# A Trainium2 kernel of attention and feed-forward layers: GpSimd's feed-forward operations tile by tile, attention's sums cleared there, a norm moved behind the last inner tile

## What is computed

```python
# layer 1: a mixture of experts on x (two of eight experts), gives x1
# layer 2: linear attention with kv sums, then this feed-forward part
x2 = layer_norm(x1 + attn, g1, b1)
gate = x2 @ Wg + bg                  # 256 -> 682
up = x2 @ Wu + bu
ffn = (silu(gate) * up) @ Wd + bd    # 682 -> 256
y = x + layer_norm(x2 + ffn, g2, b2)
# layer 3: softmax attention, 16 heads of 16, keys that the mask marks are left out
q, k, v = y @ Wq.T, y @ Wk.T, y @ Wv.T
scores = where(mask, -inf, q k^T * scale)
out = softmax(scores) v
# then Wo, an RMS norm, shift and scale by the condition
# layer 4: a mixture of experts with 16 experts and a shared one, added to y
```

## Time and profile before

| what | value |
|---|---|
| median of 3 runs | 913.29 us (911.43 to 913.87) |
| profiled execution | 911.58 us, its span 909.9 us |
| PE busy | 821.8 us (90%) |
| DVE busy | 695.6 us (76%) |
| POOL busy | 398.4 us (44%) |
| ACT busy | 362.5 us (40%) |
| granted TensorE clock, mean | 0.96 |

### The profile page before, as it was taken

The page is one execution under the profiler, slowest core; times in us unless marked ns, Lnnn a source line. Parts: engine busy times, 40 slices in busy tenths (PEclk is TensorE's granted clock), DMA queues, the critical chain, the costliest instruction groups (busy, mean ns, idle before and its releaser), DMA issues. The chain is left out here.

```text
span 909.9 us, 17077 instructions
## 1 busy us (share of the span) xinstructions
PE 821.8 (90%) x5386; PEld 736.3 (81%) x5386; DVE 695.6 (76%) x1399; ACT 362.5 (40%) x722; POOL 398.4 (44%) x435
## 2 busy tenths in 40 slices
PE   7799999999994688769999889887999999999997
PEld 4699999999994567657887779865888888888887
DVE  4888888888882578887788879787686777777776
ACT  5466655566650555243331545683111111111110
POOL 4277777877773300036654436502232333323232
PEclk9899999999997699788999999999999999999999
DMA  8436314223512600007000020010000010010002
GB/s 292 130 98 202 127 46 123 62 64 124 174 44 81 201 0 1 1 0 222 1 1 1 1 71 1 3 35 1 18 28 24 17 35 17 17 35 17 17 0 93
DMA packets 45912, 55.20 MB, mean 61 GB/s; under 512 B 5166, under 2 KB 34920, under 8 KB 45864
## 3 DMA queue, kind: packets, MB, share of 16 engines
q1 hardware_dynamic: 41384, 43.59, 15.2%
q0 software_dynamic: 4032, 11.02, 3.9%
q10 hardware_dynamic: 448, 0.01, 0.0%
HBM read 47.00 MB, written 7.60 MB: 60 GB/s over the span
## 5 line engine op out<-in xcount | busy, mean ns | idle before, releaser
L2109 POOL TENSOR_TENSOR kTh<-at_acc,kTh 128x512 fp32r<-128x512 f32 x68 | 88.1, 1295 | 231.9 <-DVE kTh L2224 231.9
L1892 PE MATMUL psum<-act_hi,ff_w 128*128 128x512 f32 x544 | 180.3, 392 | 0.4 <-ACT at_acc L2057 0.4
L2057 ACT ACTIVATE at_acc<-psum 128x512 f32<-128x512 f32 x68 | 40.6, 599 | 237.4 <-PE psum L1892 237.4
L1892 PEld LDWEIGHTS psum<-act_hi,ff_w 128*128 128x128 f32 x544 | 102.6, 189 | 21.1 <-ACT at_acc L2057 0.8
L1933 PEld LDWEIGHTS psum<-ff_w,kTh 128*128 128x128 f32 x816 | 106.4, 190 | 8.8 <-DVE y L2305 3.2
L2305 DVE SCALAR_TENSOR_TENSOR y<-psum,ff_rawd,y 128x256 f32<-128x256 f32 x272 | 112.2, 475 | 0.2 <-issue 0.2
L1933 PE MATMUL psum<-ff_w,kTh 128*128 128x256 f32 x816 | 108.4, 283 | 3.1 <-DVE y L2305 3.1
L1892 PE MATMUL psum<-act_lo,ff_w 128*128 128x512 f32 x272 | 106.9, 393 | 0.0
L470 ACT ACTIVATE e_u<-psum,e_bias 128x256 f32<-128x256 f32 x152 | 63.5, 471 | 95.3 <-PE psum L375 84.2
L2221 DVE TENSOR_TENSOR at_acc<-psum,at_acc 128x512 f32<-128x512 f32 x68 | 47.0, 691 | 71.0 <-PE psum L1892 58.6
L774 PE MATMUL psum<-act_hi,ff_w 128*128 128x512 f32 x192 | 64.7, 412 | 6.2 <-DVE ff_h32sb L1506 4.5
(11 more groups left out here) (444 smaller groups left out, 2335.4 us busy)
## 6 DMA issues: line engine op xcount, KB each, us to landing
e_raw<-in_W SPq DMA_DIRECT2D x16, 512.0 KB, 6.5
e_raw<-in_W SPq DMA_DIRECT2D x8, 1024.0 KB, 5.8
v_tok<-in_xT SPq DMA_DIRECT2D x4, 512.0 KB, 9.4
y<-in_x SPq DMA_DIRECT2D x4, 512.0 KB, 10.2
y<-y_rows SPq DMA_DIRECT2D x4, 512.0 KB, 7.3
v_tok<-y_rows SPq DMA_DIRECT2D x4, 512.0 KB, 8.1
v_tok<-in_x SPq DMA_DIRECT2D x4, 512.0 KB, 7.5
e_raw<-in_w_gate SPq DMA_DIRECT2D x16, 128.0 KB, 2.2
```

Source lines behind the costliest of these rows:

```text
L1892: last = pe.matmul(bank[:, :], e2_w[par][a][:, o + k * H2:o + (k + 1) * H2], actT[b][:, k, g * GT:(g + 1) * GT], start=n == 0, stop=n == 3 ...
L2057: act.activation(sl_sb[:, s % 2, :], ps[s % 2][:, :], ACT.Silu).then_inc(esil, 1)
L2109: pool.tensor_tensor(hh[1][:, s % HS, :], h32[:, s % 2, :], hh[0][:, s % HS, :], ALU.subtract).then_inc(hsp, 1)
```

## The change

GpSimd's operations over four tiles in the feed-forward stage (bias and shift rows, the third group's gain and join) become four operations over one tile each, with the signal on the last; the low halves of the key and value weights become two each. The third group's gain and join wait for all 24 low parts (`hsp`) and all shift adds, and the weights' low halves move behind the second join of the last group. TensorE turns the third group behind the third tile of the last `down` instead of the second, and ScalarE's and VectorE's splits of it move with it. The sums of attention are cleared in the feed-forward stage, one of 16 parts after each low part of steps 6 to 21, and their last column is written at the stage's end; TensorE's wait in attention counts that. Query products 4, 5 and 6 go to banks 4, 5 and 3 instead of 3, 4 and 5, and the wait for VectorE's split of part 3 moves from the start of attention's loop to ahead of part 6. Some small tiles are placed inside others, and `acc` is allocated for the whole kernel (not shown).

```diff
--- before.py
+++ after.py
@@ query_bank @@
-            return ps[(0, 1, 2, 3, 3, 4, 5, 7)[u]]
+            return ps[(0, 1, 2, 3, 4, 5, 3, 7)[u]]
@@ stage_feed_forward, tensor: down(g) @@
                             last.then_inc(ops, 1)
                             if g == L1 - 1 and j == 0:
                                 count_keys()
-                            if g == L1 and j == 1:
+                            if g == L1 and j == TG - 2:
                                 turn(g - 1)
@@ stage_feed_forward, scalar @@
                         act.activation(rstd[:, i:i + 1], rstd[:, i:i + 1], ACT.Sqrt).then_inc(root, 1)
-                        if i == L1 * TG + 1:
+                        if i == NT - 2:
                             hi(L1 - 1)
@@ stage_feed_forward, gpsimd @@
                         if g == 1 and m == 2:
                             constants()
+                        if FC <= s < NS - 2:
+                            pool.memset(at.acc[:, s - FC, :, :], 0.0).then_inc(cleared, 1)
                         if m % 2 and s < 4 * G:
 
                             r = s // 2 // 2
-                            sl = slice(r * TG, (r + 1) * TG)
                             if s // 2 % 2 == 0:
                                 pool.wait_ge(gin, 48)
-                                pool.tensor_tensor(y[:, sl, :], y[:, sl, :], group_rows(gb[:, 2, :]), ALU.add).then_inc(biased, 1)
+                                for i in range(r * TG, (r + 1) * TG):
+                                    last = pool.tensor_tensor(y[:, i, :], y[:, i, :], gb[:, 2, :], ALU.add)
+                                last.then_inc(biased, 1)
                             else:
                                 pool.wait_ge(xin[r], 16)
-                                pool.tensor_tensor(xk[:, sl, :], xk[:, sl, :], group_rows(gb[:, 1, :]), ALU.add).then_inc(xbiased, 1)
-                    sl = slice((L1 - 1) * TG, L1 * TG)
+                                for i in range(r * TG, (r + 1) * TG):
+                                    last = pool.tensor_tensor(xk[:, i, :], xk[:, i, :], gb[:, 1, :], ALU.add)
+                                last.then_inc(xbiased, 1)
                     pool.wait_ge(scaled, L1)
-                    pool.tensor_tensor(y[:, sl, :], y[:, sl, :], group_rows(gb[:, 0, :]), ALU.mult).then_inc(gained, 1)
+                    pool.wait_ge(xbiased, G)
+                    pool.wait_ge(hsp, NS)
+                    for i in range((L1 - 1) * TG, L1 * TG):
+                        last = pool.tensor_tensor(y[:, i, :], y[:, i, :], gb[:, 0, :], ALU.mult)
+                    last.then_inc(gained, 1)
                     pool.wait_ge(gained, 1)
-                    pool.wait_ge(xbiased, L1)
-                    pool.tensor_tensor(y[:, sl, :], y[:, sl, :], xk[:, sl, :], ALU.add).then_inc(joined, 1)
-                    for n, home in enumerate((at.wk, at.wv)):
-                        pool.wait_ge(at.weights, n + 1)
-                        pool.tensor_tensor(home[1], pj_raw[:, n + 1, :, :], home[0], ALU.subtract).then_inc(at.wsp, 1)
-                    pool.wait_ge(xbiased, G)
+                    for i in range((L1 - 1) * TG, L1 * TG):
+                        last = pool.tensor_tensor(y[:, i, :], y[:, i, :], xk[:, i, :], ALU.add)
+                    last.then_inc(joined, 1)
                     for j in range(TG - 1):
+                        if j == TG - 2:
+                            for n, home in enumerate((at.wk, at.wv)):
+                                pool.wait_ge(at.weights, n + 1)
+                                for k in range(KC):
+                                    last = pool.tensor_tensor(home[1][:, k, :], pj_raw[:, n + 1, k, :], home[0][:, k, :], ALU.subtract)
+                                last.then_inc(at.wsp, 1)
                         i = L1 * TG + j
                         pool.wait_ge(spread, j + 1)
                         pool.tensor_tensor(y[:, i, :], y[:, i, :], xk[:, i, :], ALU.add).then_inc(joined, 1)
+                    pool.wait_ge(at.penned, 1)
+                    pool.wait_ge(cleared, NI)
+                    pool.tensor_tensor(at.acc[:, :, :, HD].rearrange("p (b u) h -> p b u h", b=B),
...
@@ stage_feed_forward, vector @@
                         norm_last(j)
-                        if j == 1:
+                        if j == TG - 2:
                             lo(L1 - 1)
@@ stage_attention, tensor @@
-                        if i < 2:
-                            pe.wait_ge(qlo, j * QB + QB + i + 1)
+                        if i == 0:
+                            pe.wait_ge(qlo, j * QB + NQP - 1)
...
-                        if i == 0:
-                            pe.wait_ge(qlo, j * QB + NQP - 1)
...
-                    pe.wait_ge(at.ready, B + 1)
+                    pe.wait_ge(at.ready, B + 2)
                     n_blocks = live_blocks(pe)
                     with pe.Fori(0, n_blocks) as j:
                         pe.wait_ge(added, j * NI + 2)
-                        pe.wait_ge(qlo, j * QB + QB)
                         pe.wait_ge(ptc, j * NI + 2)
                         for u in range(QB, QB + KC):
                             query_product(pe, wq, u, qps)
                         project_keys(j)
                         project_values(j, 0)
+                        pe.wait_ge(qlo, j * QB + QB)
                         query_product(pe, wq, NQP - 2, qps)
@@ stage_attention, gpsimd @@
-                    pool.memset(acc[:, :, :, :], 0.0).then_inc(cleared, 1)
-                    pool.wait_ge(at.penned, 1)
-                    pool.wait_ge(cleared, 1)
-                    pool.tensor_tensor(acc[:, :, :, HD].rearrange("p (b u) h -> p b u h", b=B),
...
```

More of the change, by code:

```diff
@@ L1268, in stage_feed_forward @@
             at_ones, counts_ps, seen = (sem(f"ff_{x}") for x in ("ones", "countsps", "seen"))
-            gained, joined, inverted, spread = (sem(f"ff_{x}") for x in ("gained", "joined", "inverted", "spread"))
+            cleared, gained, joined, inverted, spread = (sem(f"ff_{x}") for x in ("cleared", "gained", "joined", "inverted", "spread"))
             n0 = turns_done[0]
@@ L1494, in _ @@
                         pool.tensor_tensor(y[:, i, :], y[:, i, :], xk[:, i, :], ALU.add).then_inc(joined, 1)
+                    pool.wait_ge(at.penned, 1)
+                    pool.wait_ge(cleared, NI)
+                    pool.tensor_tensor(at.acc[:, :, :, HD].rearrange("p (b u) h -> p b u h", b=B),
+                                       at.pen[:, :].unsqueeze(1).unsqueeze(3).to_broadcast([P, B, QT, NH]),
+                                       at.one[:, 0:1].unsqueeze(2).unsqueeze(3).to_broadcast([P, B, QT, NH]), ALU.mult).then_inc(at.ready, 1)
                 @block.vector
@@ L1646, in stage_attention @@
         def stage_attention(q_hi, homes, mask_rows, mask_home, v_tok, wq, qps, qhi, at, load_ahead, pre, loaded, e2_raw, e2_in):
-            mb_set, cleared = sem("at_maskset"), sem("at_cleared")
+            mb_set = sem("at_maskset")
+            acc = at.acc
             qlo, wk, wv, q_lo, z, ks, pT, xt = at.qlo, at.wk, at.wv, at.q_lo, at.z, at.ks, at.pT, at.xt
@@ L1679, in stage_attention @@
                 mb = sbl("at_mb", [P, QT, KB], BF16)
-                acc = sbl("at_acc", [P, NI, NH, HD + 1])
                 mn, df, rc = (sbl(f"at_{x}", [P, NI, NH]) for x in ("mn", "df", "rc"))
@@ L2061, in _ @@
                 def _(pool):
-                    pool.memset(acc[:, :, :, :], 0.0).then_inc(cleared, 1)
-                    pool.wait_ge(at.penned, 1)
-                    pool.wait_ge(cleared, 1)
-                    pool.tensor_tensor(acc[:, :, :, HD].rearrange("p (b u) h -> p b u h", b=B),
-                                       at.pen[:, :].unsqueeze(1).unsqueeze(3).to_broadcast([P, B, QT, NH]),
-                                       one[:, 0:1].unsqueeze(2).unsqueeze(3).to_broadcast([P, B, QT, NH]), ALU.mult).then_inc(cleared, 1)
-                    pool.wait_ge(cleared, 2)
                     def move(j, i):
@@ L2353, in adaln_block @@
         kept, mid = KC * B * HC * KB, KC * T
+        mask_end = [(rows_of.stop - rows_of.start) * (S // 4) for rows_of in mask_rows]
+        raw_line = [v[:, :, :].rearrange("p k n -> p (k n)") for v in ff_raw]
+        lists = top2[:, :, :].rearrange("p i n -> p (i n)")
         at_homes = (ff_raw[0][:, :, :].rearrange("p k n -> p (k n)"), ff_raw[1][:, :, :].rearrange("p k n -> p (k n)"), rawd_line)
@@ L2359, in adaln_block @@
             own8, own4 = sb("at_own8", [P, HC]), sb("at_own4", [P, HB])
-            rank, keys, lv, rb, srt = (sb(f"at_{x}", [P, NKB]) for x in ("rank", "keys", "lv", "rb", "srt"))
-            cnt, pen, nl = sb("at_cnt", [P, QT]), sb("at_pen", [P, QT]), sb("at_nl", [P, 1])
+            keys, lv, rb, srt = (lists[:, n * NKB:(n + 1) * NKB] for n in range(4))
+            rank, cnt, pen = (raw_line[0][:, o:o + n] for o, n in ((mask_end[0], NKB), (mask_end[0] + NKB, QT), (mask_end[0] + NKB + QT, QT)))
```

(4 more changed lines are left out.)

## The result

The changed kernel took 905.67 us (median of 6 runs, 903.81 to 907.32); the kernel before, beside it on the same chip, took 912.59 us (911.43 to 913.96). The ratio is 0.9924, 95% interval 0.9906 to 0.9941: 6.9 us less. The forecast was 907.0 with 903.0 to 912.0, and faster. The profiled execution took 907.32 us with a span of 905.6, the slowest of the six.

A forecast was written before the change was run, and what follows sets the result against it. TensorE sets the feed-forward stage, so only its holes, waits on VectorE, count. +1.1 - 1.5 - 2.4 - 2.85 - 0.65 = -6.3 us takes 911.58 to 905.3, or 907.0 on the median's scale; range 903.0 to 912.0.

The forecast's parts named there:

- A: Group 0, ahead of the first inner product: split GpSimd adds lengthen its queue, +1.1 us (bounds 0 and +1.4).
- B: Group 1, hole at 456.3: VectorE gets turns between short adds, and the later 0.4 us hole goes, -1.5 us.
- C: Group 2, hole at 485.3: same chain shortens the hole and the clock stays up behind it, -2.4 us.
- D: Last group: with the norm behind all low parts, the second query product no longer waits, -2.85 us.
- E: Attention's start: TensorE's first product no longer waits for VectorE's L805 to end, -0.65 us (bounds 0 and -0.75).
- one hole near 1 us: Expected sign ahead of the first inner product: a new hole near 1 us; above 2 us the prediction is wrong.
- The clears: Feed-forward stage: 16 small GpSimd clears, 5 us where it idles 56, taken as nothing beyond B and C.
- The first (the split buys nothing): Groups 1 and 2: GpSimd's queued adds run through, VectorE waits for all four; 911.7 us, chance 0.13.
- The second (the low clock moves): New or shifted holes bring a half-clock stretch, 1.5 us each, perhaps twice; 908.5 to 910.0 us, chance 0.20.
- The third rival: Last group: VectorE's turns stretch the norm's eight operations, TensorE's turn waits, 1.6 us comes back; 908.6 us, chance 0.10.
- The fourth (each handover loses 0.2 us): Short GpSimd operations and clears each lose 0.2 us, all felt by TensorE: +12, 919 us, chance 0.07.
- a handover of about 115 ns: Some eight handovers of the shared resource in A to C would add 0.9 us, making 907.9; left out.

The follow-up runs named there:

- experiment 6: The changed kernel with group 0's two row adds (bias and shift) wide again, one operation each: 904.82 us, ratio 0.9908 against the kernel before.
- Experiment 10: The changed kernel with VectorE's first attention signal ahead of its loading of the block count instead of behind it: 906.50 us, ratio 0.9942 against the kernel before.
- experiment 1: The kernel before with only the eight bias and shift row adds split tile by tile: 908.93 us, ratio 0.9959.
- the three parts alone: The kernel before with only the row adds split (908.93 us), only the third group's norm and turn moved (908.47), or only attention's wait and banks changed (911.98).

## Why the prediction was right, point by point

From the profiled execution's 911.58 us the sum gave 905.3, 6.3 us less. Laid over each other at the stage's start, the traces differ by 6.37 us at attention's first product and by 6.43 at the end. Mechanism and size were right part by part, with the misses named below. (The lower end of the range counts another 4 us for A, B and C, where their own bounds add up to 3.5.)

**A, forecast +1.1, measured +0.82.** The queue on GpSimd was read rightly, and the wide group 0 of experiment 6 takes back 0.85. The short operations alone were priced at 0.8; the 0.3 added for the fourth hidden tile isn't seen in the sum, though 0.82 is itself good only to a few tenths. The cost doesn't stand in one hole near 1 us, as the prediction's signs had it, but in two: 0.53 us ahead of an up product and 0.36 ahead of the first inner product.

**B, forecast -1.5, measured -1.58.** The hole shrank by 1.39 where 1.15 was forecast, the 0.4 us hole went as said, and the inner product came 3.08 us behind the up product.

**C, forecast -2.4, measured -2.53.** The hole gave 1.42 (forecast 1.15), the full clock behind it 1.34 (3.10 us from the up product to the inner product instead of 4.44; forecast 1.54, less the 0.3 for a late low part). About 0.2 us came back until the first up product behind down(2); what that is was not followed.

**D, forecast -2.85, measured -2.88.** Cast and low part took 0.43 and 0.69 us, the last multiply waited for its up product alone, and the norm ended 0.9 us before its transposes (forecast 0.8).

**E, forecast -0.65, measured -0.35,** of which 0.15 is lost between the start of the last down and the end of the stage, so the table shows -0.20; what took it was not followed. The mechanism was right and the term too large: TensorE starts 0.39 us after L805 does, a limit that the trace of before could not show, and the prediction took a value near the other end of its bounds. Experiment 10 shows that the signal isn't what is left.

**The clears, forecast nothing beyond B and C, measured 1.04.** B and C did count the clear ahead of the adds. They did not count that a clear behind a low part lengthens the held cast (1.68 us, above the 1.2 that the prediction gave as the most). On the other side the two holes came out 0.79 and 0.75 us where the forecast left 1.0 each. Two misses of opposite sign, each near half a microsecond, stand inside B and C.

**The rivals.** The first (the split buys nothing) fell on the cast of 0.81 us. The second (the low clock moves) did not happen in either trace of the changed kernel, where D has closed the hole of 2.58 us; experiment 1, with this hole open, shows it happening at 1.47 us. That D is the reason rests on that one trace. The two parts are not independent: the three parts alone give 3.88 + 2.82 + 0.45 = 7.15 us from I to T, near the 7.19 of the whole, but only since the first contains a low stretch (1.47 lost) that the whole doesn't have, and lacks the clears (1.04) that it has. With both put in the parts come to 7.6. That the sum of parts agreed is partly chance. The third rival (the turn waits) fell on the margin of 0.9 us. The fourth (each handover loses 0.2 us): alone, a group's four adds take 2.82 us, the cast 0.43, L1251 1.22 and L1252 at least 1.08, 5.55 or more in all; taking turns, everything from the first add's start to the last add's end took 4.96. An operation that was held ends sooner after its release than a free one takes: the later adds after about 0.6 us (free 0.73), L1251 after 1.08 (free 1.22).

The prediction weighed a handover of about 115 ns, which the Trainium skill's page "SBUF — State Buffer", section "A bandwidth-pool intuition that's wrong", gives for a DMA whose descriptors GpSimd can't write while VectorE holds the ports, and which made 907.9. The held cast of 457.99 ended 0.28 us behind the end of the clear, as the earlier trace rows had 0.29; no run here shows the extra. The sum without it came out at 6.3 against 6.37, but with misses of half a microsecond in it, so the sum alone would not decide.

**The median.** The profiled spans differ by only 4.3 us, since this execution of the changed kernel reached the stage 2.2 us later. The medians differ by 6.9, near the 6.43 of the stage and all behind it. The runs of one kernel spread over 3.5 us; of the changed kernel's, those at 903.8 and 904.0 us have a mean granted clock of 0.966, the profiled one 0.958.

## What to carry to other kernels

Ask of a long GpSimd operation not only how wide it is but which VectorE operation it meets: where none is due, leave it wide (0.4 us less per operation here); where one is due, even a small one with two SBUF inputs, move it, or split it so that VectorE gets in between. Even a 0.3 us clear costs time behind an operation that holds VectorE. Judge a gain near 1.4 us in one trace only after counting the low-clock stretches on both sides, and close the next hole too, or the loss can move there.

## What the runs showed of the hardware that was not expected

- **Low clock comes in portions.** Each stretch behind the stage's start cost about 1.7 us of full clock, some 1.4 us of time. The same idle may or may not start one: in the kernel before 2.17 us had one behind it, 2.18 and 2.58 us had none; in experiment 1 the 2.58 us had one; the 3.3 us at attention's start was followed by none, one or two portions in different kernels. The Trainium skill, page "TensorE: Matmul & The Clock Gate", section "Part 1: The HAM clock gate", has the chip watch TensorE's activity by a count that runs free of the kernel's start. The trace agrees so far as equal holes, shifted in time, were hit in one kernel and spared in another; the count itself no run here shows.
- **Turns are by instruction, but not always taken.** Between four short adds VectorE got in after each one. But behind the low part of 457.83 the clear of 459.06 ran too before the cast was let through (1.68 us against 1.43 without it). The Trainium skill's page "SBUF — State Buffer", section "SBUF: two separate sides", has whoever starts first hold the pair for the whole instruction; the rows agree. Why the clear kept its place while the adds gave it up was not settled.
- **Splitting is not free.** 1024 wide 2.41 us, four of 256 undisturbed 2.82, and 4.96 when three VectorE operations take turns with them.
